# State space layer: sums of step rates over later tokens as two fp32r products in place of one f32 product

## What is computed

```python
zxbcdt = x @ W_in
z, xBC, dt = ...                       # 256, 512 and 4 columns
xBC = silu(causal_conv(xBC, 4 taps) + conv_b)
dt = softplus(dt + dt_bias)
dA = exp(dt * -exp(A_log))             # one rate per token and head
h = h * dA_t + (dt_t * x_t) B_t        # scan over the tokens
y_t = h C_t
y = rmsnorm((y + D_skip * x) * silu(z)) * gnorm_w @ W_out
```

## Time and profile before

| What | Value |
|---|---|
| median of three timed executions | 1247.31 us |
| span of the profiled execution | 1250.8 us |
| PE / PEld busy | 1122.6 us (90%) / 929.6 us (74%) |
| DVE / ACT / POOL busy | 918.1 (73%) / 846.5 (68%) / 531.3 us (42%) |
| L2329, matmul passes | 44, median 526 ns (two a group) |
| L2292, matmul passes in one bank | 264, median 369 ns |

### The profile page before, as it was taken

One profiled execution on the slowest core, in us unless ns is written; L12 is line 12 of the kernel. 1 busy time (PEld: TensorE's weight loads), 2 busy tenths in 40 slices (PEclk: granted clock), 3 DMA queues, 4 the chain that ended last, 5 costly groups with the idle time before them and its releaser, 6 DMA issues. The chain is left out here.

```text
span 1250.8 us, 29697 instructions
## 1 busy us (share of the span) xinstructions
PE 1122.6 (90%) x8717; PEld 929.6 (74%) x8717; DVE 918.1 (73%) x2770; ACT 846.5 (68%) x2821; POOL 531.3 (42%) x885
## 2 busy tenths in 40 slices
PE   8999989999998999887398689997899899869996
PEld 5678767888887888777287567785788788658884
DVE  0388856999977689966565487885899788655774
ACT  1388867787885555557253478887788499736895
POOL 0368874534403278866252643222441111033552
PEclk9899988999999999988599699999999999959998
DMA  7200002321110000001522200000543000034441
GB/s 289 96 2 3 2 1 53 94 83 66 64 52 23 1 2 2 1 1 34 196 65 47 73 9 6 6 2 1 137 121 101 13 2 2 3 100 117 137 138 48
DMA packets 50825, 68.54 MB, mean 55 GB/s; under 512 B 8100, under 2 KB 30904, under 8 KB 50424
## 3 DMA queue, kind: packets, MB, share of 16 engines
q1 hardware_dynamic: 44552, 55.23, 14.6%
q0 software_dynamic: 4432, 6.59, 2.0%
q10 hardware_dynamic: 1696, 4.98, 1.0%
HBM read 60.16 MB, written 6.71 MB: 53 GB/s over the span
## 5 line engine op out<-in xcount | busy, mean ns | idle before, releaser
L497 DVE TENSOR_TENSOR f_parts<-T,f_parts 128x512 fp32r<-128x512 f32 (+1 forms) x240 | 180.1, 789 | 21.7 <-ACT f_parts L481 19.9
L473 ACT ACTIVATE T<-quad_bank,f_b1s 128x512 f32<-128x512 f32 (+1 forms) x240 | 150.4, 648 | 43.0 <-PE quad_bank L444 33.7
L444 PE MATMUL quad_bank<-XP,f_wp 128*128 128x512 f32 (+1 forms) x720 | 167.0, 377 | 0.2 <-ACT T L473 0.2
L444 PEld LDWEIGHTS quad_bank<-XP,f_wp 128*128 128x128 f32 x720 | 127.4, 191 | 25.5 <-issue 0.8
L481 ACT ACTIVATE f_parts<-T 128x512 fp32r<-128x512 f32 (+1 forms) x240 | 132.5, 592 | 0.0
L964 ACT ACTIVATE a_late<-quad_bank,a_shift 108x108 f32<-108x108 f32 x352 | 119.0, 358 | 3.2 <-DVE a_shift L1033 2.2
L457 PE MATMUL bank<-f_parts,f_wp 128*128 128x512 f32 (+1 forms) x480 | 117.1, 380 | 4.5 <-DVE XT L506 2.0
L457 PEld LDWEIGHTS bank<-f_parts,f_wp 128*128 128x128 f32 x480 | 86.1, 193 | 23.2 <-DVE XT L506 2.7
L386 POOL TENSOR_TENSOR f_wp<-f_ws,const 128x512 fp32r<-128x512 f32 (+1 forms) x32 | 33.9, 1058 | 121.8 <-DMA f_ws<-in_f_w 59.4
L768 POOL TENSOR_TENSOR a_ve<-a_mv,const 108x1 f32<-108x1 f32 x44 | 8.4, 191 | 162.7 <-DVE a_mv L1090 161.9
L964 ACT ACTIVATION_READ_ACCUMULATOR a_late<-quad_bank,a_shift 108x1 f32 x352 | 75.4, 214 | 0.0
(11 more groups left out here) (470 smaller groups left out, 3164.4 us busy)
## 6 DMA issues: line engine op xcount, KB each, us to landing
a_late<-f_gates SPq DMA_DIRECT2D x64, 256.0 KB, 3.2
a_wqk<-in_a_wqk SPq DMA_DIRECT2D x24, 256.0 KB, 2.7
f_ws<-in_f_w SPq DMA_DIRECT2D x16, 256.0 KB, 3.8
pats<-in_patches SPq DMA_DIRECT2D x5, 648.0 KB, 9.8
pats<-in_patches ACTq DMA_DIRECT2D x5, 648.0 KB, 15.0
a_wo<-in_a_wo SPq DMA_DIRECT2D x24, 128.0 KB, 2.1
a_late<-f_gates SPq DMA_DIRECT2D x16, 128.0 KB, 3.5
f_w1a<-in_f_w SPq DMA_DIRECT2D x1, 2048.0 KB, 10.7
```

The costliest lines, as they stand in the source:

```text
L444: mm = pe.matmul(self.m.quad_bank[:, q % 4, 0:w], self.wp[0][:, e % 2, a, c * 128:(c + 1) * 128], self.xp[:, b, t0:t0 + w], start=((a, b) ...
L473: act.activation(self.full[:, q % 4, 0:w], self.m.quad_bank[:, q % 4, 0:w], self.func, bias=self.b1s[:, e * self.chunks + c:e * self.chunk ...
L497: dve.tensor_tensor(self.lo[:, q % self.ring, 0:w], self.full[:, q % 4, 0:w], self.hi[:, q % self.ring, 0:w], ALU.subtract).then_inc(self. ...
```

## The change

The rates are split once into a high part (what fp32r holds) and a rest. VectorE masks the high part, ScalarE the rest with four activations per group, and TensorE adds two fp32r products in the same bank. The stationary matrix gets an fp32r copy, `later`, made once by ScalarE.

```diff
-        cum = sb("cum", [P, 2, NS, P])
+        cum = sb("cum", [P, 2, 2, NS, P], F32R)
+        later = sb("later", [P, P], F32R)
+        rate_high, rate_low = sb("rate_high", [P, G * 8], F32R), sb("rate_low", [P, G * 8])
@@ tensor @@
+            pe.wait_ge(later_ready, 1)
             for t in range(last):
                 if (g := group(t, 1)) is not None:
                     pe.wait_ge(cum_ready, g + 1)
                     at_least(pe, decay, g)
-                    pe.matmul(seg_bank[0:P, 0:NS * P], m.later, cum[:, g % 2, :, :].rearrange("p n j -> p (n j)"),
-                              start=True, stop=True).then_inc(seg_psum, 1)
+                    pe.matmul(seg_bank[0:P, 0:NS * P], later[:, :], cum[:, g % 2, 0, :, :].rearrange("p n j -> p (n j)"),
+                              start=True, stop=False)
+                    pe.wait_ge(low_ready, g + 1)
+                    pe.matmul(seg_bank[0:P, 0:NS * P], later[:, :], cum[:, g % 2, 1, :, :].rearrange("p n j -> p (n j)"),
+                              start=False, stop=True).then_inc(seg_psum, 1)
@@ scalar, ahead of the two exponentials @@
+            act.activation(later[:, :], m.later, ACT.Copy).then_inc(later_ready, 1)
             act.activation(a_exp[:, :], m.small("A_log"), ACT.Exp).then_inc(exped, 1)
@@ scalar, in the loop, behind the Square @@
                     act.activation(sq[:, :], yz[:, g % 2, :], ACT.Square, scale=1.0 / 16, accum_out=ssq[:, g % 2, :]).then_inc(ssq_ready, 1)
+                if (g := group(t, 0)) is not None:
+                    if g == 0:
+                        act.wait_ge(rates_split, 1)
+                    at_least(act, seg_psum, g - 1)
+                    for n in range(NS):
+                        a = act.activation(cum[:, g % 2, 1, n, :], m.upto, ACT.Identity, scale=rate_low[:, g * 8 + n:g * 8 + n + 1])
+                    a.then_inc(low_ready, 1)
                 if (g := group(t, 5)) is not None:
@@ vector, ahead of the loop @@
+            then(dve.tensor_copy(rate_high[:, :], m.DTA[:, :]))
+            dve.tensor_tensor(rate_low[:, :], m.DTA[:, :], rate_high[:, :], ALU.subtract).then_inc(rates_split, 1)
@@ vector, in the loop @@
-                    dve.tensor_tensor(cum[:, g % 2, :, :], m.upto.unsqueeze(1).broadcast_to([P, NS, P]),
-                                      m.DTA[:, g * 8:g * 8 + NS].unsqueeze(2).broadcast_to([P, NS, P]), ALU.mult).then_inc(cum_ready, 1)
+                    dve.tensor_tensor(cum[:, g % 2, 0, :, :], m.upto.unsqueeze(1).broadcast_to([P, NS, P]),
+                                      rate_high[:, g * 8:g * 8 + NS].unsqueeze(2).broadcast_to([P, NS, P]), ALU.mult).then_inc(cum_ready, 1)
```

More of the change, by code:

```diff
@@ L2153, in state_phase @@
         cum_ready, seg_psum, decay = sem("cum_ready"), sem("seg_psum"), sem("decay")
+        later_ready, rates_split, low_ready = sem("later_ready"), sem("rates_split"), sem("low_ready")
         z_psum, z_tanh, z_ready = sem("z_psum"), sem("z_tanh"), sem("z_ready")
```

## The result

The changed kernel takes 1298.85 us (median of 4 runs, 1297.86 to 1307.85) against 1247.03 us: 1.0387 times the kernel before, 95% interval 1.0348 to 1.0426, slower. A second series gave 1.0405 (1.0379 to 1.0430). The forecast was 1296.5 us, range 1281 to 1312. The span of the profiled execution is 1297.2 us, 46.4 more than before. The medians differ by more, 51.8 us, since the profile of the kernel before lies in an execution longer than its median (span 1250.8 against 1247.03); these 5 us are in no trace, and what follows accounts for the 46.4.

A forecast was written before the change was run, and what follows sets the result against it. TensorE, busy 90% of the span, was taken as the bound. The present 1247.3 us, plus 37.2 for iterations lengthened by the wait for ScalarE's masks, plus 12 for clock falls, gave 1296.5 us, range 1281 to 1312.

The forecast's parts named there:

- full iterations with the first ones: Token-group iterations 0 to 15, with whole convolutions: period from 5.58 to 7.43 us, with small additions +32.2 us together.
- half iterations: Iterations 16 to 19, with half convolutions: 5.92 us each, 23.7 instead of 18.64 for four, +5.0 us.
- last two and the end: The last two groups, without convolution: 12.3 us against 12.34 now, so 0, within 1 us.
- the clock: TensorE falling to 1.2 GHz in every second full-length stall, 11 or 12 times at 1.0 us: +12 us, between 0 and 25.
- The masks: ScalarE's four new activations per group: 0.37 us each, starts 0.28 apart, 1.21 us for four.
- the rival of a second operand per partition: Slower masks on ScalarE, 1.64 us for four instead of 1.21: +9.5 us, 1306 to 1315 us in all; chance 0.17.
- The ring: Loop of convolution, evictions, Square, masks, low product, the rest, next convolution: full iterations take 7.43 us instead of 5.58.
- One of the signs that were named: ScalarE's idle before its first eviction of a convolution tile (L2390) would get shorter by little.
- The low product: TensorE's second fp32r product per group, 432 columns, behind the wait for ScalarE's masks: 0.216 us.
- The covers: VectorE's fp32r mask, its two new instructions (some 0.7 us) and ScalarE's copy of `later` (about 0.25) would cost nothing.
- The rival without falls: Same TensorE stall in the token groups, clock kept at 2.4 GHz: 1284.5 us; chance 0.27.
- The other side: Masks ready in time, TensorE keeps its gain of 0.29 us in 22 groups, 6.3 us: 1241 us; chance 0.02.

The follow-up runs named there:

- e9: Changed kernel plus four idle products ahead of each high product, filling TensorE's stall (a repeat run): ratio 1.0306 to the kernel before, stage 177.4 us.
- e1: Changed kernel with ScalarE's four masks moved ahead of its evictions of the convolution piece: ratio 1.0024 to the kernel before, stage 141.6 us.
- e4: Changed kernel with the four masks moved between ScalarE's evictions and its Square: ratio 1.0250 to the kernel before, stage 175.2 us.
- e3: Changed kernel with each group's four masks also written to a spare tile, eight in all: ratio 1.0826 to the kernel before, stage 241.9 us.
- e5: Changed kernel with its wait for the masks kept, but the old f32 product instead of two fp32r ones: ratio 1.0611 to the kernel before, stage 212.6 us.

## Why the prediction was right

By its own steps, with the falls taken out by e9:

| Step | predicted, us | measured, us |
|---|---|---|
| full iterations with the first ones | +32.2 | +32.2 (31.1 between the first and the 16th L2344, 1.1 ahead) |
| half iterations | +5.0 | +5.1 |
| last two and the end | 0, within 1 | -0.9 |
| sum without the clock | +37.2 | +36.4 |
| the clock | +12 (11 or 12 falls of 1.0) | +10.7 (8 falls, six of them of 1.5) |
| stage | +49.2 | +47.1 |

**The masks.** 376 ns each and 1.20 to 1.21 us for four, against 0.37 and 1.21; the rival of a second operand per partition is out. The row of the masks:

```profile
L2459 ACT ACTIVATE ss_cum<-const,ss_rate_low 108x108 fp32r<-108x108 f32 x88 | 26.4, 376 | 0.0
```

**The place.** The ring is the predicted one, element by element: 2.77 to the first eviction (predicted 2.79), 1.03 to the Square (1.02), 0.39 (0.40), masks 1.21, 0.05 (0.06). e1 and e4 show it by moving the masks, e3 by doubling them, e5 by keeping the wait with the old product. One of the signs that were named came out the other way: ScalarE's idle ahead of the first eviction did not get shorter, it is 2.83 us where it was 2.60.

**The low product.** 502.99 - 502.70 = 0.29 us, not 0.216. The wait makes the difference: in e1, where it doesn't wait, the pair takes 0.26 to 0.27 and then 0.19 to 0.20 in the full iterations, 0.46 together. So it costs 0.07 more than forecast in 22 groups, 1.6 us, hidden in the sum by errors the other way. The figure of the Trainium skill (TensorE: Matmul & The Clock Gate, Back-to-back issue gap), 0.183, would have been further off.

**The covers.** The mask of VectorE takes 576 to 604 ns into fp32r; the f32 one took 576 to 609 in 14 groups and 1.02 us in the eight where POOL's xd (the product of x and D, one of its eight steps) ran well beside it. ScalarE's copy is not seen. But VectorE's two additions ahead of the loop (0.25 and 0.34 us) were put at nothing, behind the first stall, and are not covered by it. The loop's first eviction waits for VectorE's gating, not for its convolution, which starts at 416.53:

```profile
419.89 0.62 ACT L2397 ACTIVATE ss_cv<-bank,ss_half 128x432 f32<-128x432 f32 x1 [3.50 <-DVE ss_sx L2473]
```

That is 3.36 us behind the start of the convolution, where 2.79 were forecast: 0.57 late, and the masks with it. From that convolution to the first L2344 it is 5.9 us in e9, where the kernel before had 3.32, so 2.6 more and not 1.98. That the table has only 1.1 ahead of the first L2344, and its first row agrees to the digit, is luck: the kernel before had the slow stretch of 412.98 in the convolutions ahead of the loop, the changed one has none there, and so this convolution starts 18.7 us into the stage instead of 20.2. (In e4, with such a stretch at 412.80, it starts after 20.2 again, and the eviction comes 2.78 behind it.)

**The clock.** Right in kind; the sum is near by luck, with two errors that cancel: too many falls, too low a price. At 1.0 us each I had a quarter of a slow stretch hidden in a stall; in the windows above the slow stretch begins behind a stall and is all work (3.42 of 3.42 busy), so that the full 1.4 to 1.5 is paid. The Trainium skill (the same page, Why this matters for your kernels), by which such short pauses would not slow the clock, is contradicted here: ahead of the eight falls TensorE sat idle for 1.85 to 2.65 us at a time, and filling the stalls (e9) kept the clock at 1.00. Why other stalls of the same length (1.99 us from 476.35) are not followed by a fall is left open. The rival without falls, 1284.5, is what e9 measures: 1.0306 x 1247 = 1285.

**The other side.** The gain of 6.3 us if the masks were in time was too high even as a rival: e1 had them in time and gained nothing, since POOL's loop, 5.63 us in the mean of four turns, was no faster than TensorE's 5.57.

## What to carry to other kernels

Work given to an engine that is half idle costs what its place in that engine's list costs: find what stands ahead of it, what that waits for, and whether the consumer comes earlier; here the same four instructions cost 46 us behind the evictions and nothing ahead of them. A regular stall on TensorE is paid twice, by itself and through the clock, so before taking work off a busy engine list the next loop too, with its longer turns (here 5.63 us in the mean against 5.57), and open that first.

## What was not expected of the hardware

- The clock's falls came in a fixed pattern: both profiles of the changed kernel, from two series, have eight in the stage at the same places within 0.4 us, and the same stage of 188.1 us.
- Idle products made the kernel faster: about 1.56 us of them in each of 22 groups took 10.7 us off.
- With stalls of 3.1 to 3.7 us (e3) what is put down to the clock is 29 us more than in the changed kernel, more than the doubled masks themselves, and once the clock stayed down for 51 us while TensorE still did more than five iterations.
- A product behind a wait cost more than in a stream: 0.29 instead of 0.216 us (fp32r, 432 columns), 0.15 + 0.78 instead of 0.72 (f32, two passes).
- VectorE's mask and POOL's xd, when they overlap in time (e1, 467.85 and 467.35), take 1.02 and 1.05 us; apart, in most groups of the changed kernel, 0.60 and 0.61. That they hold each other up was not tried by itself.
